# Fetching the basis matrices of a graph network base by base, in whole blocks, instead of by strided transfers over all bases

## The chip, the cores and the metric

The kernel runs on one core of one Trainium2 chip. The metric is the device time of one execution in microseconds (us). The profiled execution has a span of its own, from the first to the last instruction, and a time of its own beside it.

## What is computed

The reference is four layers on 10000 nodes of width 512 with 5000 edges: a relational graph network of two layers, a mixture-of-experts feed-forward, a second graph network of four layers, and a quantized feed-forward. The change touches only what prepares the first of them. Its two relations use weights that are combined from 30 bases:

```
x = x + gnn(layernorm(x), edges, basis1, att1, ..., basis2, att2, ...)
def rgcn_gate_layer(x, row, col, edge_type, basis, att, gate_w, root, bias):
    w = jnp.einsum('rb,bio->rio', att, basis)      # att 2x30, basis 30x512x512, w 2x512x512
```

There are two such tensors of bases (one for each layer), each 30 x 512 x 512 floats, 31.5 MB; together 62.9 MB that have to come from DRAM once.

## The kernel before

The kernel is a chain of phases with a barrier of all engines between them. The change is in the first large one, `front_phase` (line 230), which does three things side by side:

- It normalizes the rows of the input: `load(g)` (line 355) fetches 256 rows (512 KB) into one of four buffers, VectorE takes their statistics (`stats`, line 474, through `row_stats`, line 149), GpSimd makes the factors (`rstd`, line 317), ScalarE applies them and stores 512 KB to `normed` (`norm`, line 384). There are 40 such groups, the last of 16 rows.
- It sorts the edges by node, in 40 turns on TensorE, VectorE and GpSimd (`counts`, `turn_hot` and `look` from line 577, `advance` and `ranks` on VectorE, `scatter` on GpSimd).
- It combines the bases: for each of the two layers the 512 rows are cut into 8 blocks of 64 rows (`SIDE`, `BLOCKS`), 16 blocks in all. A block of all 30 bases lies in the on-chip memory with 120 partitions: base b has the partitions 4b to 4b+3, and partition 4b+q holds the rows q, q+4, q+8, ... of the block. Sixteen matrix products (`term`, line 548, one for each of the 16 rows of a partition) add up into one bank (`cb_ps`), the stationary operand (`spread`) putting row 4k+q of both relations in its place. ScalarE and VectorE split the result into a high and a low part (`block_high`, `block_low`), and ScalarE's queue stores both, 256 KB each.

SyncE issues all loads in an order written out by hand (lines 332 to 365). A block of bases comes as two halves, a half as four transfers, one for each quarter q: each reads, of all 30 bases, 8 rows that stand four rows apart, and writes 30 partitions that stand four apart, 480 KB in pieces of 2 KB. There are 32 halves in four buffers, so 128 transfers. A half waits (line 350) until the block that used its buffer is done. After the first four halves, each turn of the loop issues the load of one group of input rows, which waits for the `norm` of the group three before (line 357), and then on average 0.7 halves:

```
    src_ = networks[n][0].rearrange("b (j k q) o -> j b q k o", j=BLOCKS, q=4)[b]
    for quarter in range(4):
        eng.dma_start(ba_t[i % W][quarter:BASIS_ROWS:4, :, :], src_[:, quarter, half * HALF:(half + 1) * HALF, :]).then_inc(ba[i % W], 16)
```

TensorE's order is written by hand too: the 16 terms of block 0, the histogram of the edges, the terms of block 1, and then in every turn of the sort some 5.6 terms (lines 563 to 603). It waits for the bases at the first term of each half (line 550). ScalarE's queue has the stores of `normed` and of the combined weights (lines 392 and 404). After the sort SyncE reads back the sorted table (line 370), and the phase ends some 10 us later; the next phase, `relation_phase`, starts with its own loads (line 735 on).

Other transfers that the text behind this section speaks of: the loads of the edge lists on 125 partitions (line 336), the store of the gate's probabilities from 16 partitions (line 1119), the load of the edge terms on 5 partitions (line 1711), and the loads of the combined weights (line 743).

Of the kernel before, what the change touches and what calls it, by code (L numbers as in the profile page):

```python
# [10 lines left out]
P = 128  # L11
N, D, E = 10000, 512, 5000
KC = D // P
RELATIONS, BASES = 2, 30
# [7 lines left out]
ET = -(-E // P)  # L22
# [6 lines left out]
def wait(eng, sem, value):  # L29

    if not isinstance(value, int) or value > 0:
        eng.wait_ge(sem, value)  # L32
# [191 lines left out]
SIDE = 64  # L224
SHARE = SIDE // 4
BASIS_ROWS = 4 * BASES
BLOCKS = D // SIDE

def front_phase(core, ed, cst, src, dst, kind, weight, rows_in, normed, networks, combined):  # L230
# [6 lines left out]
    W = 4  # L237
# [2 lines left out]
    names = ("ld0 ld1 ld2 ld3 st0 st1 stats aggr var rstd nb norm "  # L240
             "ints rows hilo hot hist histc scan off base put "
             "count turned ohT look val rank made zdone tab fin1 wide place heads lasts merged "
             "att0 att1 ba0 ba1 ba2 ba3 cb chi clo cs0 cs1 sw0 sw1")
    with core.phase("order", names) as (s, sbuf, psum):
        load_i = sbuf("load_i", [P, 5, ET], I32)
        col = sbuf("col", [P, 5, ET])
# [29 lines left out]
        mv = [sbuf(f"mv{q}", [P, TILES, 2]) for q in range(W)]  # L276
        rs, ng, nb = ([sbuf(f"{n}{q}", [P, TILES]) for q in range(W)] for n in ("rs", "ng", "nb"))
        ld, st = [s[f"ld{q}"] for q in range(W)], [s[f"st{q}"] for q in range(2)]
        HALF = SHARE // 2
        ba_t = [sbuf(f"basis{q}", [BASIS_ROWS, HALF, D]) for q in range(W)]  # L280
        spread = [sbuf(f"spread{n}", [BASIS_ROWS, P + SIDE - 4]) for n in range(2)]
        c_hi, c_lo = [sbuf(f"c_hi{q}", [P, D], F32R) for q in range(2)], [sbuf(f"c_lo{q}", [P, D], F32R) for q in range(2)]
        ba, cs = [s[f"ba{q}"] for q in range(W)], [s["cs0"], s["cs1"]]
        ct_ps = [psum(f"ct_ps{q}", [HI, D]) for q in range(2)]
        c_ps = [a[:, 0:KEYS * P].rearrange("a (k p) -> a k p", k=KEYS) for a in ct_ps]
        turn_ps = [a[:, KEYS * P:KEYS * P * 3 // 2].bitcast(BF16).rearrange("a (k p) -> a k p", k=KEYS) for a in ct_ps]
# [8 lines left out]
        cb_ps = [psum(f"cb_ps{q}", [P, D]) for q in range(2)]  # L295
# [7 lines left out]
        with nc.Block() as block:  # L303
            @block.gpsimd
            def _(eng):
                eng.memset(load_i[:, 0:2, :], PAD_NODE)
                eng.memset(load_i[:, 2, :], RELATIONS)
                eng.memset(load_i[:, 3:5, :], 0)
                eng.memset(wt[:, :], 0.0)
                for n in range(2):  # L310
                    eng.memset(spread[n][:, :], 0.0)
                for k in range(KEYS):
                    eng.memset(row_i[k][:, E:EP], PAD_NODE)
                eng.memset(ones[:, :], 1.0)
                eng.memset(zeros[:, :], 0.0).then_inc(s["made"], 1)

                def rstd(g):
                    q = g % W
                    n, k = (REST, 1) if last(g) else (P, TILES)
                    wait(eng, s["norm"], g - W + 1)  # L320
                    row_rstd(eng, s, g, mv[q], cst.half, rs[q], last(g))
                    eng.wait_ge(s["rstd"], g + 1)
                    eng.tensor_tensor(nb[q][0:n, 0:k], ng[q][0:n, 0:k], rs[q][0:n, 0:k], ALU.mult).then_inc(s["nb"], 1)

                def scatter(t):
                    eng.wait_ge(s["rank"], t + 1)
                    for k in range(KEYS):
                        eng.indirect_dma_start(ed.table[k], bass.IndirectOffsetOnAxis(ap=ix[:, k, t:t + 1], axis=0),
                                               packed[:, k, t, :], None).then_inc(s[f"sw{k}"], 16)
                static_pipeline([(0, rstd), (2, scatter)], ET)  # L330

            @block.sync
            def _(eng):
                eng.wait_ge(s["made"], 1)
                for j, a in enumerate((src, dst, kind, src, dst)):
                    eng.dma_start(load_i[0:USED, j, :], a.rearrange("(p t) -> p t", t=ET)).then_inc(s["ints"], 16)
                eng.dma_start(wt[0:USED, :], weight.rearrange("(p t) one -> p (t one)", t=ET)).then_inc(s["ints"], 16)
                for n, (_, att) in enumerate(networks):
                    for r in range(RELATIONS):
                        for quarter in range(4):  # L340
                            at = SIDE - 4 + r * SIDE + quarter
                            eng.dma_start(spread[n][quarter:BASIS_ROWS:4, at:at + 1], att[r].rearrange("(b one) -> b one", one=1),
                                          allow_slow_non_contiguous=True).then_inc(s[f"att{n}"], 16)
                for k in range(KEYS):
                    eng.dma_start(row_i[k][:, 0:E], key_in[k].partition_broadcast(P)).then_inc(s["rows"], 16)
                eng.dma_start(ed.sums[1][ZERO_ROW:SUM_ROWS, :], zeros[:, :]).then_inc(s["zdone"], 16)

                def basis(i):
                    n, b, half = i // (2 * BLOCKS), i // 2 % BLOCKS, i % 2
                    wait(eng, s["cb"], (i - W) // 2 + 1 if i >= W else 0)  # L350
                    src_ = networks[n][0].rearrange("b (j k q) o -> j b q k o", j=BLOCKS, q=4)[b]
                    for quarter in range(4):
                        eng.dma_start(ba_t[i % W][quarter:BASIS_ROWS:4, :, :], src_[:, quarter, half * HALF:(half + 1) * HALF, :]).then_inc(ba[i % W], 16)

                def load(g):
                    q = g % W
                    wait(eng, s["norm"], g - W + 1)
                    eng.dma_start(part(x[q], last(g)), rows(rows_in, g, last(g))).then_inc(ld[q], 16)
                halves = 2 * 2 * BLOCKS
                for i in range(W):  # L360
                    basis(i)
                for t in range(ET):
                    load(t)
                    for i in range(min(halves, W + halves * t // ET), min(halves, W + halves * (t + 1) // ET)):
                        basis(i)

                for k in range(KEYS):
                    eng.wait_ge(s[f"sw{k}"], 16 * ET)
                for k in range(KEYS):
                    eng.dma_start(tabT[:, k, :, :], ed.table[k].rearrange("(t p) c -> t p c", p=P)).then_inc(s["tab"], 16)  # L370
                eng.wait_ge(s["tab"], 16 * KEYS)
                eng.wait_ge(s["wide"], KEYS)
                for k in range(KEYS):
                    eng.dma_start(ed.key_row[k].rearrange("(t p) -> t p", p=P), lineT[:, k, :]).then_inc(s["fin1"], 16)
                eng.wait_ge(s["wide"], KEYS + 2)
                for j, row in enumerate((weight_hi.ap().bitcast(F32), weight_lo.ap().bitcast(F32), weight_hi.ap().bitcast(F32),
                                         ones.ap(), ones.ap())):
                    eng.dma_start(ed.weight_rows[j].rearrange("(t p) -> t p", p=P), row).then_inc(s["zdone"], 16)
                eng.wait_ge(s["zdone"], 16 * (1 + TERMS))
                eng.wait_ge(s["fin1"], 16 * KEYS)  # L380
# [165 lines left out]
            @block.tensor  # L546
            def _(eng):
                def term(n, b, k):
                    j, half = n * BLOCKS + b, k // HALF
                    if k % HALF == 0:  # L550
                        i = 2 * j + half
                        eng.wait_ge(ba[i % W], (i // W + 1) * 64)
                    if k == 0:
                        if b == 0:
                            eng.wait_ge(s[f"att{n}"], 16 * RELATIONS * 4)
                        wait(eng, s["clo"], j - 1)
                    at = SIDE - 4 - 4 * k
                    m = eng.matmul(cb_ps[j % 2][:, :], spread[n][:, at:at + P], ba_t[(2 * j + half) % W][:, k % HALF, :],  # L558
                                   start=k == 0, stop=k == SHARE - 1)
                    if k == SHARE - 1:  # L560
                        m.then_inc(s["cb"], 1)
# [4 lines left out]
                for k in range(KEYS):  # L566
                    for t in range(ET):
                        m = eng.matmul(h_ps[:, k, :], hot_hi[k][:, t, :], hot_lo[k][:, t, :], start=t == 0, stop=t == ET - 1)
# [4 lines left out]
                for k in range(KEYS):  # L573
                    m = eng.matmul(o_ps[:, k:k + 1], cst.after[0:HI, 0:HI], incl[:, k, P - 1:P], start=True, stop=True)
# [30 lines left out]
                for k in range(KEYS):  # L605
                    m = eng.transpose(w_ps[:, k, :], apart[:, k, :], cst.ident[0:HI, 0:HI])
# [4 lines left out]
                for k in range(KEYS):  # L611
                    m = eng.matmul(m_ps[:, k, ET:ET + 1], shift[:, :], lineT[:, k, P - 1:P], start=True, stop=True)
                m.then_inc(s["lasts"], 1)
                for k in range(KEYS):
                    for c in range(3):
                        m = eng.transpose(t_ps[:, k, c, :], tabT[:, k, :, c], cst.ident[0:ET, 0:ET])
# [844 lines left out]
def routed_phase(core, cst, rows_in, w1, b1, w2, b2, token, score, routed):  # L1461
# [4 lines left out]
    K = HID + 1  # L1466
    HALF = SL * TPE // 2 + 2 - SL * TPE // 2 % 2
    names = ("w whi wlo ix T hi lo hm act gh gl one O ev "
# [934 lines left out]
```

## Time and profile before

| | |
|---|---|
| median of 3 runs | 5509.27 us (5506.63 to 5516.06) |
| profiled execution: time | 5506.21 us |
| profiled execution: span | 5504.4 us |
| mean granted TensorE clock | 0.827 |
| TensorE (matmul) busy | 4216.8 us, 77% of the span |
| VectorE, ScalarE, GpSimd busy | 2992.2, 2139.4, 1455.9 us |
| bytes moved by DMA | 924.32 MB, mean 168 GB/s |
| the phase of the change | from the start to about 463 us |

The profile's page cuts the span into 40 slices of 137.6 us; the phase of the change fills the first three and a third. A busy digit is in tenths. The DMA share is that of the core's 16 DMA engines, each packet counted for the time from its start to its end. In a row of a timeline the first number is the start, the second the duration. KB are of 1024 bytes, MB and GB of powers of ten.

### The profile page before, as it was taken

How to read it: one execution, taken by the hardware profiler on the slowest of the kernel's cores; microseconds unless marked ns; L12 is line 12 of the kernel's file. 1: busy time of each engine (PE TensorE's matmuls, PEld its weight loads, DVE VectorE, ACT ScalarE, POOL GpSimd, SP SyncE). 2: the span in 40 equal slices, each digit the busy share in tenths (PEclk: the TensorE clock that was granted, in tenths of full speed). 3: DMA queues.
4: the chain of work that ended last, by engine and by line, in shares of the span. 5: the costliest groups of instructions: out<-in, count | busy, mean ns of one | idle time of the engine just before them, and what ended most of it. 6: DMA issues, size and time to landing. Idle time of an engine off the chain costs nothing. (4 is left out here: it accounts for less than half of the span.)

```text
span 5504.4 us, 70253 instructions
## 1 busy us (share of the span) xinstructions
PE 4216.8 (77%) x22571; PEld 3378.6 (61%) x22571; DVE 2992.2 (54%) x6700; ACT 2139.4 (39%) x3450; POOL 1455.9 (26%) x1380
## 2 busy tenths in 40 slices
PE   5766989799897710663389897989889897989533
PEld 2334868688786610542179773988579774988311
DVE  3435754377685564434755445554455435554588
ACT  0111213222337800220133564347533664347566
POOL 1322112211340007774433004310233004310243
PEclk9887999899998855665589995999789995999755
DMA  8994237722896603666955226532555127532354
GB/s 235 295 273 152 77 114 250 238 72 71 330 401 244 235 20 90 121 127 157 330 177 162 76 94 231 162 112 91 194 171 162 72 96 234 162 106 92 136 195 161
DMA packets 493679, 924.32 MB, mean 168 GB/s; under 512 B 107759, under 2 KB 108039, under 8 KB 492632
## 3 DMA queue, kind: packets, MB, share of 16 engines
q1 hardware_dynamic: 296076, 532.11, 29.2%
q0 software_dynamic: 118272, 237.34, 15.8%
q10 hardware_dynamic: 79088, 151.77, 7.6%
q8 instruction: 136, 2.23, 0.2%
q14 instruction: 107, 0.88, 0.0%
HBM read 597.24 MB, written 322.46 MB: 167 GB/s over the span
## 5 line engine op out<-in xcount | busy, mean ns | idle before, releaser
L684 PE MATMUL hidden_O<-hidden_xh,w_hi 128*128 128x256 f32 (+1 forms) x2560 | 728.8, 285 | 0.3 <-DVE hidden_xl L1057 0.2
L685 PE MATMUL hidden_O<-hidden_xh,w_lo 128*128 128x256 f32 (+1 forms) x2560 | 717.0, 280 | 0.0
L686 PE MATMUL hidden_O<-hidden_xl,w_hi 128*128 128x256 f32 (+1 forms) x2560 | 716.8, 280 | 0.0
L684 PE MATMUL output_O<-w_hi,output_hh 128*128 128x512 f32 (+1 forms) x1264 | 503.3, 398 | 56.5 <-DVE output_hl L1950 56.5
L1829 POOL DMA_INDIRECT hidden_agg<-edge_sums,edge_where x316 | 339.6, 1075 | 756.8 <-DVE hidden_xin L1876 605.6
L1860 ACT ACTIVATE hT<-hidden_O,hidden_b 128x256 f32<-128x256 f32 (+1 forms) x640 | 247.6, 469 | 659.1 <-PE hidden_O L686 659.1
L685 PE MATMUL output_O<-w_hi,output_hl 128*128 128x512 f32 (+1 forms) x1264 | 502.4, 397 | 0.0
L686 PE MATMUL output_O<-w_lo,output_hh 128*128 128x512 f32 (+1 forms) x1264 | 502.1, 397 | 0.0
L684 PEld LDWEIGHTS hidden_O<-hidden_xh,w_hi 128*128 128x128 f32 x2560 | 484.4, 189 | 1.5 <-DVE hidden_xl L1057 1.4
L685 PEld LDWEIGHTS hidden_O<-hidden_xh,w_lo 128*128 128x128 f32 x2560 | 485.2, 190 | 0.0
L686 PEld LDWEIGHTS hidden_O<-hidden_xl,w_hi 128*128 128x128 f32 x2560 | 483.3, 189 | 0.0
L1956 DVE TENSOR_TENSOR output_y<-output_O,output_b2t 128x1024 f32<-128x1024 f32 (+1 forms) x160 | 193.7, 1211 | 510.9 <-PE output_O L686 510.9
L1882 DVE BATCH_NORM_STATS2 h_stats<-hT 128x6 f32<-128x256 f32 (+1 forms) x640 | 221.1, 408 | 447.0 <-ACT hT L1860 447.0
L1732 POOL DMA_INDIRECT message_x<-g,edge_partner x160 | 174.5, 1091 | 821.8 <-issue 722.0
L558 PE MATMUL order_cb_ps<-order_basis,order_spread 120*128 120x512 f32 x512 | 269.2, 680 | 79.1 <-DMA order_basis<-in_L_gnn_basis 79.1
L1966 ACT ACTIVATE hT<-hT,output_shf,output_scl (+2 forms) x640 | 326.7, 581 | 0.0
L684 PEld LDWEIGHTS output_O<-w_hi,output_hh 128*128 128x128 f32 (+1 forms) x1264 | 237.6, 188 | 116.1 <-issue 56.7
L686 PEld LDWEIGHTS output_O<-w_lo,output_hh 128*128 128x128 f32 (+1 forms) x1264 | 237.4, 188 | 60.3
L685 PEld LDWEIGHTS output_O<-w_hi,output_hl 128*128 128x128 f32 (+1 forms) x1264 | 237.7, 188 | 59.8
L1774 PE MATMUL message_X<-message_attr_terms,message_edge_terms 5*128 5x512 f32 x160 | 125.1, 787 | 186.8 <-DMA message_attr_terms<-edge_attr_rows 183.2
L684 PE MATMUL root_O<-root_hi,root_xh 128*128 128x512 f32 (+1 forms) x632 | 254.1, 402 | 0.0
L684 PE MATMUL relation_B<-w_hi,relation_pth 128*128 128x512 f32 x640 | 253.6, 396 | 0.0
(376 smaller groups left out, 10014.4 us busy)
## 6 DMA issues: line engine op xcount, KB each, us to landing
hidden_xin<-g SPq DMA_DIRECT2D x156, 512.0 KB, 4.0
g<-output_y SPq DMA_DIRECT2D x156, 512.0 KB, 2.7
order_basis<-in_L_gnn_basis SPq DMA_DIRECT2D x128, 480.0 KB, 16.5
edge_sums<-message_res SPq DMA_DIRECT2D x160, 256.0 KB
edge_sums<-relation_res SPq DMA_DIRECT2D x80, 256.0 KB, 2.0
order_x<-in_x SPq DMA_DIRECT2D x39, 512.0 KB, 17.9
normed<-order_y ACTq DMA_DIRECT2D x39, 512.0 KB, 9.2
root_xin<-normed SPq DMA_DIRECT2D x39, 512.0 KB, 3.7
```

What stands on the lines that cost most here:

```text
L558: m = eng.matmul(cb_ps[j % 2][:, :], spread[n][:, at:at + P], ba_t[(2 * j + half) % W][:, k % HALF, :], start=k == 0, stop=k == SHARE - 1)
L684: eng.matmul(out, a_hi, b_hi, start=start, stop=False)
L685: eng.matmul(out, a_lo, b_hi, start=False, stop=False)
L686: return eng.matmul(out, a_hi, b_lo, start=False, stop=stop)
L1732: eng.indirect_dma_start(x[t % R][:, :], None, table, bass.IndirectOffsetOnAxis(ap=ed.partner[1][:, t:t + 1], axis=0)).then_inc(ga[t % R], 16)
L1774: eng.matmul(X[t % 2][:, :], edge_terms[:, t * P:(t + 1) * P], attr_terms[:, :], start=True, stop=True).then_inc(s["E"], 1)
L1829: eng.indirect_dma_start(agg[j % R][0:n, :], None, ed.sums[1], bass.IndirectOffsetOnAxis(ap=ed.where[1][0:n, c:c + 1], axis=0)).then_inc(g ...
L1860: m = eng.activation(hT[:, o, at(g)], O[g % 2][:, o, 0:width_of(last(g))], ACT.Identity, bias=b1t[:, o:o + 1])
L1882: m = eng.bn_stats(stats[:, o, g, :], hT[:, o, at(g)])
L1956: eng.tensor_tensor(part(y[q], last), part(O[q], last), b2t[0:n, :].unsqueeze(1).to_broadcast([n, k, D]), ALU.add).then_inc(s["add"], 1)
L1966: m = eng.activation(hT[:, o, at(g, w_)], hT[:, o, at(g, w_)], ACT.Relu, bias=shf[:, o:o + 1], scale=scl[:, o:o + 1])
```

## The change

The buffers are two, each for a whole block, in place of four for half a block; their total size is the same. A block of bases is fetched by 30 transfers, one for each base, each of which reads 64 neighbouring rows of the base (128 KB in one piece of DRAM) and writes them to the four partitions of that base. There are 480 transfers in place of 128. A block waits once, at its first base, until the block before the last is done. The first two blocks are issued ahead of the first load of input rows; the other 14 are cut into 70 pieces of six transfers and spread evenly over the 40 turns. TensorE waits once per block, for all 30 transfers.

```diff
-        HALF = SHARE // 2
-        ba_t = [sbuf(f"basis{q}", [BASIS_ROWS, HALF, D]) for q in range(W)]
+        ba_t = [sbuf(f"basis{q}", [BASIS_ROWS, SHARE, D]) for q in range(2)]
...
-        ba, cs = [s[f"ba{q}"] for q in range(W)], [s["cs0"], s["cs1"]]
+        ba, cs = [s["ba0"], s["ba1"]], [s["cs0"], s["cs1"]]
...
-                def basis(i):
-                    n, b, half = i // (2 * BLOCKS), i // 2 % BLOCKS, i % 2
-                    wait(eng, s["cb"], (i - W) // 2 + 1 if i >= W else 0)
-                    src_ = networks[n][0].rearrange("b (j k q) o -> j b q k o", j=BLOCKS, q=4)[b]
-                    for quarter in range(4):
-                        eng.dma_start(ba_t[i % W][quarter:BASIS_ROWS:4, :, :], src_[:, quarter, half * HALF:(half + 1) * HALF, :]).then_inc(ba[i % W], 16)
+                def basis(j, b0, b1):
+                    n, i0 = j // BLOCKS, j % BLOCKS * SIDE
+                    if b0 == 0:
+                        wait(eng, s["cb"], j - 1)
+                    for b in range(b0, b1):
+                        eng.dma_start(ba_t[j % 2][4 * b:4 * b + 4, :, :],
+                                      networks[n][0][b, i0:i0 + SIDE, :].rearrange("(k q) o -> q k o", q=4)).then_inc(ba[j % 2], 16)
...
-                halves = 2 * 2 * BLOCKS
-                for i in range(W):
-                    basis(i)
+                pieces = [(j, b) for j in range(2, 2 * BLOCKS) for b in range(0, BASES, 6)]
+                for j in range(2):
+                    basis(j, 0, BASES)
                 for t in range(ET):
                     load(t)
-                    for i in range(min(halves, W + halves * t // ET), min(halves, W + halves * (t + 1) // ET)):
-                        basis(i)
+                    for j, b in pieces[len(pieces) * t // ET:len(pieces) * (t + 1) // ET]:
+                        basis(j, b, b + 6)
...
                 def term(n, b, k):
-                    j, half = n * BLOCKS + b, k // HALF
-                    if k % HALF == 0:
-                        i = 2 * j + half
-                        eng.wait_ge(ba[i % W], (i // W + 1) * 64)
+                    j = n * BLOCKS + b
                     if k == 0:
+                        eng.wait_ge(ba[j % 2], (j // 2 + 1) * 16 * BASES)
...
-                    m = eng.matmul(cb_ps[j % 2][:, :], spread[n][:, at:at + P], ba_t[(2 * j + half) % W][:, k % HALF, :],
+                    m = eng.matmul(cb_ps[j % 2][:, :], spread[n][:, at:at + P], ba_t[j % 2][:, k, :],
```

## Rows read from the trace of the kernel before

**Rows 1.** The page's slices: granted clock, DMA share and rate.
```profile
PEclk9887999899998855665589995999789995999755
DMA  8994237722896603666955226532555127532354
GB/s 235 295 273 152 77 114 250 238 72 71 330 401 244 235 20 90 121 127 157 330 177 162 76 94 231 162 112 91 194 171 162 72 96 234 162 106 92 136 195 161
```
**Rows 2.** Windows: length; PE, PEld, DVE, ACT, POOL busy; PE clock, DMA share, GB/s.
```profile
34.60:453.00 418.40, 305.03 (x918) 147.35 (x918) 165.26 (x710) 69.60 (x95) 117.58 (x160) 0.86 0.95 269
50.00:350.00 300.00, 233.91 (x719) 112.42 (x717) 116.78 (x494) 49.69 (x68) 81.17 (x112) 0.87 1.01 290
```
**Rows 3.** Waits of the engines in the window 34 to 453 us.
```profile
ACT order_y L389 <- DVE order_c_lo L481: 156.2, 13, 28.3
DVE order_bn L152 <- DMA order_x<-in_x: 124.5, 20, 15.9
PE order_cb_ps L558 <- DMA order_basis<-in_L_gnn_basis: 79.1, 13, 44.8
PE order_l_ps L593 <- DVE order_junk L461: 62.9, 15, 13.7
```
**Rows 4.** The page's DMA issues: queue, count, KB each, us to landing.
```profile
order_basis<-in_L_gnn_basis SPq DMA_DIRECT2D x128, 480.0 KB, 16.5
...
order_x<-in_x SPq DMA_DIRECT2D x39, 512.0 KB, 17.9
normed<-order_y ACTq DMA_DIRECT2D x39, 512.0 KB, 9.2
```
**Rows 5.** DMA issues of the whole trace: the first of four stores of combined weights.
```profile
combined1hi<-order_c_hi ACTq DMA_DIRECT2D x8, 256.0 KB, 7.9
```
**Rows 6.** DMA in 36 to 46 us, strided basis transfers alone.
```profile
DMA packets 1121, 2.15 MB, mean 215 GB/s; under 512 B 69, under 2 KB 69, under 8 KB 1121
...
q1 hardware_dynamic: 1121, 2.15, 98.2%
```
**Rows 7.** Window 1520 to 1570 us, 256-row transfers over 128 partitions; columns of Rows 2.
```profile
1520.00:1570.00 50.00, 50.00 (x255) 42.10 (x254) 42.06 (x73) 20.42 (x24) 22.45 (x32) 1.00 1.05 406
```
**Rows 8.** Timeline of SP's queue at 2693 us; DMA in 2694.7 to 2695.59 us.
```profile
2693.86 0.28 SPq L1711 DMA_DIRECT2D message_edge_terms<-edge_weight_rows  x1
...
DMA packets 5, 0.10 MB, mean 115 GB/s; under 512 B 0, under 2 KB 0, under 8 KB 0
...
q1 hardware_dynamic: 5, 0.10, 47.6%
```
**Rows 9.** Window 5.7 to 8 us, loads over 125 partitions landing; columns of Rows 2.
```profile
5.70:8.00 2.30, 0.00 (x0) 0.00 (x0) 0.00 (x0) 0.00 (x0) 0.00 (x0) 1.00 0.31 51
```
**Rows 10.** Store from 16 partitions: its issue; DMA in 1912.4 to 1919.9 us.
```profile
1912.05 0.33 SPq L1119 DMA_DIRECT2D probs<-tokens_pT  x1
...
DMA packets 41, 0.65 MB, mean 87 GB/s; under 512 B 23, under 2 KB 23, under 8 KB 24
...
q1 hardware_dynamic: 32, 0.64, 80.1%
```
**Rows 11.** Timeline: 16 issues of 128 KB each on SP's queue.
```profile
464.64 10.36 SPq L743 DMA_DIRECT2D w_hi<-combined1hi  x16
```
**Rows 12.** Timeline: one group's way from its statistics to its norm.
```profile
208.64 1.29 DVE L152 BATCH_NORM_STATS2 order_bn<-order_x 128x6 f32<-128x512 f32 x2 [8.02 <-DMA order_x<-in_x]
209.96 0.25 DVE L156 BATCH_NORM_AGGREGATE order_mv<-order_bn 128x2 f32<-128x6 f32 x2
...
210.63 0.72 POOL L171 TENSOR_TENSOR order_rs<-order_mv,cst_half 128x2 f32<-128x2 f32 x1 [8.12 <-DVE order_mv L163]
...
211.43 0.21 POOL L323 TENSOR_TENSOR order_nb<-order_ng,order_rs 128x2 f32<-128x2 f32 x1
...
223.50 1.52 ACT L389 ACTIVATE order_y<-order_x,order_nb,order_rs 128x512 f32<-128x512 f32 x2 [16.06 <-DVE order_c_lo L481]
```
**Rows 13.** Timeline: end of the sort and read-back of the table.
```profile
446.86 0.69 DVE L481 TENSOR_TENSOR order_c_lo<-order_cb_ps,order_c_hi 128x512 fp32r<-128x512 f32 x1 [1.74 <-ACT order_c_hi L398]
...
452.92 0.95 SPq L370 DMA_DIRECT2D order_tabT<-edge_table  x2
```

More of the change, by code:

```diff
@@ L242, in front_phase @@
              "count turned ohT look val rank made zdone tab fin1 wide place heads lasts merged "
-             "att0 att1 ba0 ba1 ba2 ba3 cb chi clo cs0 cs1 sw0 sw1")
+             "att0 att1 ba0 ba1 cb chi clo cs0 cs1 sw0 sw1")
     with core.phase("order", names) as (s, sbuf, psum):
```

## The prediction

> **What bounds the kernel now.** I read the page's slices first. In the first three the DMA engines are busy 8 to 9 tenths while the rate is only 235 to 295 GB/s [rows 1]. The windows of the phase say the same: from 34.6 us, when the first basis transfer runs, to 453 us the DMA share is 0.95 at 269 GB/s, and from 50 to 350 us it is 1.01 at 290 GB/s, while TensorE, the busiest compute engine, works 305 of 418 us [rows 2]. The waits agree: VectorE waits 124.5 us for input rows, TensorE 79.1 us for bases; ScalarE's 156.2 us behind VectorE's `c_lo` is the same delay handed on, since that follows the terms [rows 3]. So this phase is bound by transfers, and the phases are separated by barriers: what it gains or loses goes to the end one for one.
>
> The bytes can be counted. Bases: 128 x 480 KB = 62.9 MB. Input rows and `normed`: 39 x 512 KB and the short group, 20.5 MB each way [rows 4]. Combined weights: four tensors like the one shown, 32 x 256 KB = 8.4 MB [rows 5]. That is 112.3 MB, and 269 GB/s x 418.4 us is 112.5.
>
> Two rates are at work. When the strided basis transfers run alone, packets of 2 KB keep the engines 98.2% busy and yield 215 GB/s, 13.5 GB/s for each of 16 [rows 6]. Transfers of 2 KB pieces over all 128 partitions yield 406 GB/s at a full share, 25.4 GB/s for each [rows 7]. With these the phase adds up: 62.9 MB / 215 = 293 us, the other 49.4 MB / 406 = 122 us, together 415 us against 418.4 [rows 2]. I use this sum for the forecast, as it has just given the time before.
>
> **What the change does, part by part.**
>
> *How many engines serve a transfer.* This decides all. The trace shows engines going by the count of the outermost dimension, not by bytes. The edge terms, 100 KB on five partitions, go as exactly five packets, each on an engine of its own [rows 8]. The loads over 125 partitions fill 0.31 of 16 engines, which is five, the largest divisor of 125 up to 16 [rows 9]. A new basis transfer has four partitions outside on the one side and q = 4 on the other: I take four engines. If always the same four, they carry every base. The Trainium skill, "DMA: Bandwidth & Descriptors", section "Why a DMA increments its semaphore by 16 and not by 1", states both: the number is the largest up to 16 that divides the slowest dimension on both sides, and from SyncE it is the lowest-numbered ones. The five packets and the 0.31 agree; that it is the same four no row here shows.
>
> *The load on those four.* Each carries 62.9 / 4 = 15.73 MB of bases instead of about 4, beside its sixteenth of the rest, 49.4 / 16 = 3.09 MB, which at 25.4 GB/s takes 122 us as now [rows 7].
>
> *The rate of each.* Nothing before streams such transfers, so I bound it. Upper end: 25.4 GB/s [rows 7]. Lower end: the store from 16 neighbouring partitions, 640 KB by 16 packets that take 0.801 x 7.5 x 16 / 16 = 6.0 us each, 6.7 GB/s per engine [rows 10]. Between: the five packets, five neighbouring partitions, 0.476 x 0.89 us x 16 / 5 = 1.36 us for 20 KB, 15.1 GB/s [rows 8], and the strided stream with 13.5 [rows 6]. Few neighbouring partitions cost rate. I take 13.5: that row is nearest in size of piece, source and duration, and the five packets lie close to it. Then the bases take 15.73 MB / 13.5 GB/s = 1165 us instead of 293, +872 us. At 15.1 they take 1042 (+749), at 25.4 619 (+326), at 6.7 2348 (+2055).
>
> In the Trainium skill, "SBUF — State Buffer", section "Door 1: The DMA port swizzle", four neighbouring partitions share one port of about 27 GB/s, so that all four engines of a transfer meet there. By that alone a transfer moves 27 GB/s and the bases take some 2300 us; only engines that have drifted into different transfers get more. Rows 10 agree (four partitions to a port, 27 GB/s); rows 8 gave more than that in a short burst.
>
> *Issues.* SyncE issues 480 instead of 128. Sixteen issues of 128 KB took 10.36 us, 0.65 us each [rows 11], so 311 us. The transfers of at least 619 us cover that; if that cover were gone (all engines at work), 311 us plus the loads would be near the bound. Cost here: nothing.
>
> *Waits of TensorE: 16 instead of 32.* It can start a block only when all of it has landed, and its 305 us of work [rows 2] lie under transfers of over 1200. Now block 0 may start at the half. This costs nothing while the transfers are the bound, except at the end, where the terms of the last block follow the last landing; they do so now too. The `cb` wait of SyncE is the same in substance (a buffer is refilled when its block is done), and what stands behind it in SyncE's order, the loads of input rows, now waits in the same queue behind 30 transfers instead of 4.
>
> *The order.* The last basis piece of a block is issued two or three turns after the turn in which TensorE starts that block, and each turn's load waits for the `norm` three turns back. So where it is three (8 of the 14 blocks) TensorE must first reach the turn, VectorE, GpSimd and ScalarE must norm its group, before the last pieces go out. That chain is 1.3 + 0.3 + 0.7 + 0.2 + 1.5 = 4 us of work [rows 12], and with issue and the way there I take 8 us. In all but two of the blocks (counted from the two lists of turns) a piece of 0.8 MB is already queued beyond, which covers it. Two times 8 us: +16 us. Bounds: 0 and 14 x 8 = 112 us.
>
> *The tail.* Now SyncE's read-back of the table starts at 452.92, six us after the last block's `c_lo` [rows 13]. That stays behind the last block.
>
> **Sum.** 872 + 16 = +888 us on the profiled execution's 5506.2 us: 6394. Its time is 3 us under the median of the runs shown, which I leave out of account. About 0.2%, 11 us, is what a measurement here can tell from no change.
>
> **The rivals.**
>
> *The four engines run apart.* If the strided stream is slow for its strides in DRAM and not for where it writes, or if the four drift into different transfers, each gives 25.4 GB/s: +326 + 16, 5848 us. For it: the new reads are one piece of 128 KB. [...] Against: the five packets, whose source is dense, are slow too [rows 8].
>
> *They meet all the time.* 6.7 GB/s each: +2055 + 16, 7577 us. For it: the order is the same on all four, and each drained queue lines them up again. Against: 15.1 in rows 8. A mixture, lined up at each block and apart after, lies between 6394 and this.
>
> *The transfers spread over all engines.* This ends faster. The place is how the 64 rows are dealt out; it decides from the point where the bases move at over 215 GB/s, which at 25.4 each needs nine engines. Then bases take 62.9 / 406 = 155 us, the rest 122, in all 277, and the next bound is SyncE's issues, 311 us and 40 loads of 0.4 us (of the size of those in rows 8 and 10): 327 instead of 415, 5418 us. For it: the bytes of a transfer are one piece in DRAM and could be cut anywhere. Against: rows 8 and 9.
>
> *The change does nothing to the time*: the engines number about nine, or the transfers are hidden; against it speaks a DMA share of 0.95 [rows 2]. 5506 us.
>
> **How the numbers follow.** Four engines at 13.5 to 15: 0.45. Apart: 0.25. Always meeting, or nearly: 0.17. Spread: 0.10. Nothing: 0.03. The forecast is the likeliest, 6394 us. The range begins just under the second case, 5830, and ends at 7300, inside the mixtures towards the third; outside stay the spread, the unchanged and the worst meeting, about 0.2. Faster 0.10, same 0.03, slower 0.87.
>
> **What would show it.** Right: the phase ends near 1340 us; in its slices the DMA share falls from 0.95 to some 0.3 while its rate falls to some 90 GB/s; TensorE's wait for `order_basis` grows from 79 to many hundred us; SyncE's basis issues stretch over the whole phase, x480 of 128 KB; the phases behind keep their length. A window with only bases shows a share near 0.25: that is the four engines; its GB/s over four is their rate, 13.5 by the forecast, 25.4 or 6.7 by the rivals. Wrong at the first step would be a share near 1 there.

## The result and the profile after

The changed kernel takes 6083.17 us (median of 4 runs, 6071.82 to 6090.84) against 5512.67 us of the kernel before in the same series: a ratio of 1.103, 95% interval 1.100 to 1.105, or 570 us slower. The forecast was 6394 us, range 5830 to 7300, with 0.87 on slower. The profiled execution took 6071.82 us; its span is 6070.0.

The page's slices of the changed kernel, 151.8 us each, to be read beside [rows 1]. In the first six and a half the DMA share is 3 to 4 tenths where it was 8 to 9, and the rate 106 to 137 GB/s:

```profile
DMA  3433334227722987225769542554255424552354
GB/s 106 136 110 116 123 114 137 73 83 247 237 73 87 392 323 271 81 71 118 128 161 321 161 135 85 186 167 134 88 177 173 143 85 166 181 149 80 121 185 166
```

Windows of the changed kernel: the phase up to the last bases, a stretch near its start with bases alone, one a little later, and a stretch of the next phase (columns of [rows 2]):

```profile
34.60:1012.00 977.40, 295.72 (x910) 143.44 (x911) 159.49 (x688) 68.29 (x93) 112.42 (x155) 0.67 0.36 114
...
36.00:46.00 10.00, 0.00 (x0) 0.00 (x0) 0.00 (x0) 0.00 (x0) 0.00 (x0) 1.00 0.26 30
60.00:100.00 40.00, 9.20 (x16) 4.05 (x17) 0.00 (x0) 0.00 (x0) 0.00 (x0) 1.00 0.26 97
...
1060.00:1160.00 100.00, 98.16 (x495) 83.44 (x496) 73.83 (x212) 25.58 (x43) 17.05 (x14) 0.96 0.24 78
```

The same bytes as before, 114 GB/s x 977 us = 111 MB, take 977 us instead of 418. With bases alone the share is 0.26 of 16 engines: four engines. The trace's semaphore events say the same: the 240 transfers into one buffer raise its semaphore 1200 times, five each: once at the issue and then once for each of four engines. That share of 0.26 holds through 60 transfers issued one behind the other. Had different transfers gone to different fours, more would have been busy at a time, so it is always the same four; that is inferred, as no packet names its engine. The phase behind runs as it did (78 GB/s; 79 in the same stretch before). The read-back of the sorted table, at 452.92 us before [rows 13], is at 1020.01: 567 us later, which is all of the difference.

The longest waits of the phase, to be read beside [rows 3]. TensorE now waits 716.3 us for bases instead of 79.1, and VectorE and GpSimd, whose share of each turn stands behind TensorE's, wait with it:

```profile
POOL order_rs L171 <- DVE order_mv L163: 858.9, 39, 146.9
PEld order_cb_ps L556 <- DMA order_basis<-in_L_gnn_basis: 725.4, 16, 90.8
PE order_cb_ps L556 <- DMA order_basis<-in_L_gnn_basis: 716.3, 16, 90.8
DVE order_ohT L470 <- PE order_ct_ps L583: 699.7, 39, 60.3
ACT order_y L389 <- DVE order_c_lo L481: 435.2, 13, 65.1
```

What the forecast did not have is in the DMA view of 36 to 76 us, one figure for each microsecond. The share doesn't move, but the rate begins at 27 GB/s, stays near 30 for 12 us and then climbs to 98:

```profile
DMA  2232222222222222222222222222222222222222
GB/s 27 25 31 39 29 27 25 41 31 25 29 47 39 37 53 78 78 76 86 76 90 74 92 78 96 78 94 92 92 98 96 92 98 94 90 96 86 98 88 94
```

So the four engines deliver anything from 7 to 25 GB/s each on the same kind of transfer. The semaphore events of the slow part show them in step: the four completions of a transfer land together, at 40.18 to 40.24 us and again at 44.30 to 44.64; from 47 us on they no longer come in fours. The slow part comes back after most pauses of the queue. This is such a pause, from the timeline of the changed kernel (start and duration in us):

```profile
415.40 3.70 SPq L352 DMA_DIRECT2D order_basis<-in_L_gnn_basis  x3
421.09 5.49 PE L556 MATMUL order_cb_ps<-order_basis,order_spread 120*128 120x512 f32 x6 [45.89 <-DMA order_basis<-in_L_gnn_basis]
...
430.83 0.68 DVE L481 TENSOR_TENSOR order_c_lo<-order_cb_ps,order_c_hi 128x512 fp32r<-128x512 f32 x1
...
432.47 1.52 ACT L389 ACTIVATE order_y<-order_x,order_nb,order_rs 128x512 f32<-128x512 f32 x2 [56.64 <-DVE order_c_lo L481]
...
434.02 0.39 SPq L358 DMA_DIRECT2D order_x<-in_x  x1
```

SyncE has issued all that it may at 419.10. The block that TensorE waits for is in at 421.09. Only then can the sort's turn go on, VectorE write `c_lo` of the block before, ScalarE, which stands behind it, norm a group at 432.47, and SyncE go on at 434.02. Fifteen us without a new transfer; by the packets of SyncE's queue, all four engines have nothing left from 428.4 to 435.0. This happens nine times in the phase, for 4.5 to 11.1 us and 63 us in all (three times and 18 us in the kernel before). The rate from 434 to 474 us, with the input rows' 244 to 410 GB/s at first, is then 43 to 91 for 14 us before it climbs (the 154 to 242 are input rows again):

```profile
GB/s 12 66 244 406 410 345 78 27 248 251 68 53 58 91 70 60 70 57 43 66 84 76 74 86 78 154 242 170 70 82 92 86 88 94 90 96 98 100 129 268
```

SyncE's waits for `norm` over the phase (46.7 us in the kernel before):

```profile
SPq L358 <- ACT order_y L389: 144.3, 11, 19.4
```

### The profile page after: what moved, and what is told of

Read it like the earlier page. It is cut to its first block and busy times, and to the rows that moved or that the text cites. A ratio compares the mean times of both kernels' runs of the same rounds, so it can differ in the third digit from the quotient of the medians.

```text
span 6070.0 us, 70605 instructions
## 1 busy us (share of the span) xinstructions
PE 4192.8 (69%) x22571; PEld 3360.7 (55%) x22571; DVE 2993.9 (49%) x6700; ACT 2142.7 (35%) x3450; POOL 1457.5 (24%) x1380
## 5 line engine op out<-in xcount | busy, mean ns | idle before, releaser
L556 PE MATMUL order_cb_ps<-order_basis,order_spread 120*128 120x512 f32 x512 | 266.9, 674 | 716.3 <-DMA order_basis<-in_L_gnn_basis 716.3
L556 PEld LDWEIGHTS order_cb_ps<-order_basis,order_spread 120*128 120x128 f32 x512 | 106.8, 218 | 843.1 <-DMA order_basis<-in_L_gnn_basis 725.4
L470 DVE CAST order_ohT<-order_ct_ps 80x256 f32<-80x256 bf16 x40 | 16.8, 420 | 699.7 <-PE order_ct_ps L583 699.7
L389 ACT ACTIVATE order_y<-order_x,order_nb,order_rs 128x512 f32<-128x512 f32 (+1 forms) x79 | 60.1, 808 | 761.9 <-DVE order_c_lo L481 435.2
```

## The experiments

My theory (A) after reading this: the loss has three parts. Four engines instead of sixteen; their meeting at the four neighbouring partitions that they all write, which begins anew after every pause and ends as they drift into different transfers; and the pauses. The rival (B): the slow stretches belong to the source in DRAM or to starting up. The next two experiments change one of these each.

### Pieces three turns earlier

```diff
-                    for j, b in pieces[len(pieces) * t // ET:len(pieces) * (t + 1) // ET]:
+                    for j, b in pieces[len(pieces) * (t + 3) // ET if t else 0:min(len(pieces), len(pieces) * (t + 4) // ET)]:
```

> The changed kernel with every piece of the bases issued three turns earlier in SyncE's order (a block still waits until the block before the last is done). Theory A, the four engines meet on one place in the on-chip memory after each pause and drift apart while their queues stay full: the pauses before the starts of blocks go, so there is only the slow stretch at the very beginning. Of the 977 us that the bases took, 741 are the four engines at 25.4 GB/s, 236 are pauses and slow stretches; some 200 of them go: about 5880 us, and the DMA share no longer falls to 0 between blocks. Rival B, the slow stretches belong to the transfers or to the source in DRAM and not to the pauses: only the pauses go, at least 6000 us.

Measured: 5901.61 us, ratio 1.071 (1.069 to 1.072); 182 us less than the changed kernel. The first stretch is nearly as slow as before, since nothing there has changed; its DMA rate in 36 to 46 us is 40 GB/s. After it SyncE hardly waits for `norm` any more (10.0 us; 144.3 in the changed kernel), its queue never runs dry, and the slow restarts are gone. The row from the waits of its queue:

```profile
SPq L358 <- ACT order_y L389: 10.0, 7, 2.6
```

The slow stretches follow the pauses, so they don't belong to the transfers. As A had it; the time is 22 us over its figure.

### The four partitions of a base four apart

Base b has the partitions 16 (b / 4) + b mod 4 + 4q in place of 4b + q. Eight partitions among the 128 then hold zeros, which VectorE writes once, and the factors of `spread` come in more and smaller loads, on ScalarE's queue.

```diff
-        ba_t = [sbuf(f"basis{q}", [BASIS_ROWS, SHARE, D]) for q in range(2)]
+        ba_t = [sbuf(f"basis{q}", [P, SHARE, D]) for q in range(2)]
...
-                        eng.dma_start(ba_t[j % 2][4 * b:4 * b + 4, :, :],
+                        p0 = b // 4 * 16 + b % 4
+                        eng.dma_start(ba_t[j % 2][p0:p0 + 13:4, :, :],
```

> The changed kernel, same transfers and same order, but the four partitions of a base stand four apart (16 partitions for four bases) instead of next to each other. Theory A, the four engines of a transfer meet because they write four neighbouring partitions: now they don't, so 36 to 46 us shows about 100 GB/s at a share of 0.25 instead of 30 GB/s, and each restart too; the pauses stay. Some 150 us less: about 5930 us. Rival B, the slow starts come from the DRAM side or from starting up: 36 to 46 us stays at about 30 GB/s and the time at about 6080 us.

Measured: 5946.55 us, ratio 1.078 (1.076 to 1.080), 137 us less than the changed kernel. The DMA view of the same 36 to 76 us, the same reads by the same four engines:

```profile
DMA  2222222222222222222222222222222222222222
GB/s 98 98 100 98 98 100 98 102 98 98 98 98 98 98 100 102 98 100 98 98 98 98 100 100 100 102 102 98 102 102 98 102 102 98 100 100 102 98 102 100
```

98 GB/s all along. This is not the stream's beginning, though: with the factors' loads gone from SyncE's queue, its bases start at about 23 us, 11 us earlier than in the changed kernel. They rise to 98 GB/s in 6 us, where the changed kernel takes some 30. The restarts decide it. This is 262 to 302 us, after 11 us without anything in the queue; the queue fills again at 264.8, and past the burst of input rows the rate is near 100 and never under 76:

```profile
GB/s 262 264 14 98 307 410 406 360 102 209 388 101 104 100 88 99 101 102 162 268 209 76 100 100 102 98 100 102 100 98 102 102 98 98 102 102 164 309 148 84
```

The reads are the same and the queue still runs dry nine times, 63 us in all, so rival B is out, and what slows the four engines is shown: that they write four neighbouring partitions at one time. Of the 137 us some 11 are the earlier start. By the Trainium skill, "SBUF — State Buffer", section "Door 1: The DMA port swizzle", four neighbouring partitions share one port of about 27 GB/s, and the first figures here are 27 and 25.

### Both together

> The changed kernel with both edits, pieces three turns earlier and the four partitions of a base four apart. Theory A, pauses and meetings are all that lies between the 741 us of four engines at 25.4 GB/s and what was measured: 741 us instead of the 415 of the kernel before, and a little at both ends, 5840 to 5880 us. Rival B, a third loss remains (the queue of SyncE, the order of the loads): no better than the earlier pieces alone, 5895 us or more.

Measured: 5873.21 us, ratio 1.066 (1.064 to 1.067). The phase from the first bases to the end of the last (columns of [rows 2]):

```profile
34.60:812.00 777.40, 328.30 (x916) 158.09 (x916) 168.07 (x701) 70.06 (x95) 113.84 (x157) 0.71 0.41 143
```

777 us against 741 (619 for the bases and 122 for the rest) of four engines that never meet nor pause. So no third loss of size is left: the 570 us are about 360 for having four engines (some 370, as this kernel too starts its bases 11 us earlier), and 200 to 210 for pauses and meetings. The two don't add up. Taking the meetings away is worth 137 us while there are pauses (6083 to 5947) but 28 without (5902 to 5873), the 11 us of the earlier start in both. The pauses are worth 182 us while the engines meet but 73 when they don't. The 73 us are close to the 63 for which the queue is dry. Some 110 us are the meetings that a pause sets off.

### Two bases per transfer

The transfer has 8 partitions on one side and 2 bases on the other. To keep it to three dimensions a partition now holds neighbouring rows (16q + k in place of 4k + q, in the stationary operand too).

```diff
-                    for b in range(b0, b1):
-                        eng.dma_start(ba_t[j % 2][4 * b:4 * b + 4, :, :],
-                                      networks[n][0][b, i0:i0 + SIDE, :].rearrange("(k q) o -> q k o", q=4)).then_inc(ba[j % 2], 16)
+                    for b in range(b0, b1, 2):
+                        eng.dma_start(ba_t[j % 2][4 * b:4 * b + 8, :, :],
+                                      networks[n][0][b:b + 2, i0:i0 + SIDE, :].rearrange("b (q k) o -> b q k o", q=4)).then_inc(ba[j % 2], 16)
```

> Two bases per transfer (256 KB in eight partitions, 240 transfers), each partition holding 16 neighbouring rows. If the engines go by the smaller outermost dimension (2 bases in DRAM, 8 partitions on chip): two engines, a share near 0.13 and at most 51 GB/s with bases alone; 31.5 MB per engine at 25.4 GB/s is 1239 us, so at least 6450 us. Rival, they go by the destination's 8 partitions: eight engines, a share near 0.5, and a time between 5500 and 5650 us.

Measured: 6453.77 us in one run. Bases alone (columns of [rows 2]):

```profile
36.00:46.00 10.00, 0.00 (x0) 0.00 (x0) 0.00 (x0) 0.00 (x0) 0.00 (x0) 1.00 0.12 52
```

Twice the bytes per transfer and twice the partitions, and half the engines: 0.12 of 16 is two. That is the count of bases; by the eight partitions it would have been eight. The semaphore events agree: three for each transfer, one at the issue and two engines'. The two write different groups of four partitions, and each gives its full 26 GB/s. By the rule in the Trainium skill, "DMA: Bandwidth & Descriptors", section "Why a DMA increments its semaphore by 16 and not by 1", the engines divide both dimensions, and 2 is what divides 8 and 2.

### Dense rows with four engines

The control for the kernel above: one base per transfer, 16 neighbouring rows (32 KB) per partition.

> The changed kernel with 16 neighbouring rows per partition: each of the four engines reads its own 32 KB piece in DRAM, where before their 2 KB rows alternated; destinations, engines and order are unchanged. Theory A, they meet at the destination: 36 to 46 us stays slow, under 50 GB/s, and the time within 60 us of the changed kernel's 6083. Rival B, they meet at the source, where four engines read alternate rows of one piece: near 100 GB/s at 36 to 46 us and a time near 5940 us.

Measured: 6040.59 us in one run, 43 us under the changed kernel, in a series whose kernel before was 14 us slower (5526.22); and 33 GB/s in 36 to 46 us:

```profile
36.00:46.00 10.00, 0.00 (x0) 0.00 (x0) 0.00 (x0) 0.00 (x0) 0.00 (x0) 1.00 0.21 33
```

The engines meet also when each reads a piece of its own. A second answer against the DRAM side, and within the 60 us that A allowed.

### One transfer per block, fifteen engines

Whole-block buffers and the earlier turns as in the first experiment, dense rows, and all 120 partitions at once.

```diff
-                    for b in range(b0, b1):
-                        eng.dma_start(ba_t[j % 2][4 * b:4 * b + 4, :, :],
-                                      networks[n][0][b, i0:i0 + SIDE, :].rearrange("(k q) o -> q k o", q=4)).then_inc(ba[j % 2], 16)
+                    if b1 == BASES:
+                        eng.dma_start(ba_t[j % 2][:, :, :],
+                                      networks[n][0][:, i0:i0 + SIDE, :].rearrange("b (q k) o -> b q k o", q=4)).then_inc(ba[j % 2], 16)
```

> The changed kernel's two whole-block buffers, the pieces' turns three earlier, but one transfer per block for all 120 partitions, each holding 16 neighbouring rows (32 KB in one piece). Outermost dimensions 120 and 30: 15 engines, a share of 0.94 or more with bases alone and over 200 GB/s there. The number of engines was then the whole loss: 5460 to 5530 us. Rival, waiting for whole blocks in two buffers costs of itself: 5560 us or more with the engines busy all the same.

Measured: 5563.97 us, ratio 1.009 (1.007 to 1.011): slower than before by some 50 us. The time is that of the rival (5560 us or more), not that of the number of engines alone. The share is near that of fifteen engines (0.94), the rate 199 GB/s:

```profile
36.00:46.00 10.00, 0.00 (x0) 0.00 (x0) 0.00 (x0) 0.00 (x0) 0.00 (x0) 1.00 0.95 199
```

So fifteen engines, with dense rows and one transfer per block, bring back 338 of the 388 us that the first experiment was slower than before. This run doesn't part the three; dense rows alone gave 43 us with four engines. The rest is not the whole-block wait alone: the kernel before with only that wait is the next experiment.

### The kernel before, waiting for whole blocks

```diff
-                    if k % HALF == 0:
-                        i = 2 * j + half
-                        eng.wait_ge(ba[i % W], (i // W + 1) * 64)
+                    if k == 0:
+                        for i in (2 * j, 2 * j + 1):
+                            eng.wait_ge(ba[i % W], (i // W + 1) * 64)
```

> The kernel before, but TensorE waits for both halves of a block at its first term. The prediction put this at nothing: within 10 us of the kernel before. Rival, TensorE then starts each block later and hands the delay on through the sort to the loads: 20 to 60 us slower.

Measured: 5518.59 us, ratio 1.0015 (1.0004 to 1.0026). It costs, but some 8 us only (interval 2 to 14), within the 10 that were expected. So the wait for whole blocks explains a small part of the 50 us of the one transfer.

### Is the kernel before held by meetings too?

This goes beyond the second experiment: no two of the fifteen write into the same four neighbouring partitions, and no run shows which engine would meet which. Four kernels ask what limits the stream. All have dense rows (the partition's rows are 16q + k) and half-block buffers, and fifteen engines but for the last:

- dense quarters: the transfers of the kernel before, 16 KB in one piece instead of eight rows of 2 KB;
- dense halves: one transfer for the four quarters, so that an engine stays 64 KB at the four partitions of a base;
- short stays: twice the transfers at half the size, 8 KB at a partition;
- ten apart: ten bases per transfer, partitions twelve apart, so ten engines. Here the factors' loads are on ScalarE's queue, and the first bases are issued at 8.4 us instead of 21.8.

```diff
-                    src_ = networks[n][0].rearrange("b (j k q) o -> j b q k o", j=BLOCKS, q=4)[b]
+                    src_ = networks[n][0].rearrange("b (j q k) o -> j b q k o", j=BLOCKS, q=4)[b]
...
-                    for quarter in range(4):
-                        eng.dma_start(ba_t[i % W][quarter:BASIS_ROWS:4, :, :], src_[:, quarter, half * HALF:(half + 1) * HALF, :]).then_inc(ba[i % W], 16)
+                    for k in range(0, HALF, 4):
+                        for quarter in range(4):
+                            eng.dma_start(ba_t[i % W][quarter:BASIS_ROWS:4, k:k + 4, :], src_[:, quarter, half * HALF + k:half * HALF + k + 4, :]).then_inc(ba[i % W], 16)
```

(The first two lines are the dense quarters, the rest the short stays.)

> The kernel before, with rows of a partition that are neighbours in DRAM: each transfer reads 16 KB in one piece from each of the 30 bases instead of eight rows 8 KB apart; partitions, engines and order unchanged. Theory A, the strided stream's 215 GB/s comes from engines that meet at their destinations: it stays near 215 GB/s in 36 to 46 us and the time within 15 us of the kernel before. Rival B, it comes from the stride of the rows in DRAM: up to 406 GB/s there, and a time of 5400 to 5440 us.

> The kernel before with dense rows, as in the dense quarters, and one transfer per half of a block instead of four (32 transfers of 1.9 MB). If number and size of the transfers don't matter beside the number of engines: as the dense quarters, 5460 to 5490 us. If the alternation of four small transfers helped the pairs of engines to drift apart: slower than that, 5490 to 5515 us.

> The dense quarters with twice as many transfers of half the size, so that an engine stays 8 KB instead of 16 KB at one group of four partitions before it goes to the next. If pairs of engines meet there and come apart sooner when the stays are short (16 KB stays: 5475 us; 64 KB stays: 5556 us): at or under 5475 us, 5440 to 5475. Rival, more and smaller transfers cost SyncE and the engines more than that: 5480 us or more.

> The kernel before with dense rows and ten bases per transfer, twelve partitions apart: ten engines, which by the rule of the partitions drawn from the second experiment never meet. Theory A: bases alone show a share of 0.63 and 254 GB/s from the first one on, above the 215 of fifteen engines in pairs; other transfers keep sixteen engines, so each of the ten carries 6.3 MB of bases and 3.1 MB of the rest, 370 us instead of 415: 5460 to 5490 us. Rival, the pairs were not what held the fifteen: ten give two thirds of 215, about 145 GB/s, and the time is 5600 us or more.

| | median, us | ratio to before (95%) | 36 to 46 us, nearly all bases | 50 to 350 us |
|---|---|---|---|---|
| before | 5512.88, 5509.57, 5526.22 in the three series | | 215 GB/s | 290 GB/s |
| dense halves, 64 KB stays (second series) | 5556.20 | 1.008 (1.007 to 1.010) | 205 | 266 |
| dense quarters, 16 KB (first) | 5474.59 | 0.993 (0.992 to 0.995) | 229 | 321 |
| short stays, 8 KB (third) | 5470.75 | 0.990 (0.989 to 0.992) | 269 | 323 |
| ten apart (third) | 5534.19 | 1.002 (1.000 to 1.003) | 262 | 278 |

The windows of 50 to 350 us, of the dense halves, the dense quarters and the short stays:

```profile
50.00:350.00 300.00, 225.15 (x680) 108.67 (x678) 110.79 (x468) 46.04 (x63) 75.59 (x105) 0.87 0.98 266
```
```profile
50.00:350.00 300.00, 241.96 (x784) 118.86 (x783) 132.39 (x563) 57.78 (x79) 92.92 (x128) 0.90 0.98 321
```
```profile
50.00:350.00 300.00, 244.18 (x785) 120.26 (x784) 135.66 (x578) 58.35 (x80) 93.92 (x131) 0.90 0.97 323
```

From 36 to 46 us, the dense quarters and the short stays:

```profile
36.00:46.00 10.00, 1.41 (x2) 0.83 (x3) 0.00 (x0) 0.00 (x0) 0.00 (x0) 1.00 0.98 229
```
```profile
36.00:46.00 10.00, 3.21 (x4) 1.51 (x5) 0.00 (x0) 0.00 (x0) 0.00 (x0) 1.00 0.96 269
```

And ten engines that by theory A never meet, with bases alone but for some tiny loads of factors:

```profile
36.00:46.00 10.00, 10.00 (x25) 4.40 (x24) 0.00 (x0) 1.28 (x1) 0.00 (x0) 1.00 0.64 262
```

Ten engines deliver more than fifteen: 26 GB/s each at a share of 0.64, in all 262 against 229 with the same dense pieces of 16 KB. So fifteen get in each other's way and ten, twelve partitions apart, don't. That they do so where they write is what the second experiment suggests; with fifteen instead of ten, though, there are also more reads at once, and no run here tells the two apart. What it is worth in time is not as A had it. The ten-apart kernel was to take 5460 to 5490 us and took 5534, which misses the rival's 5600 too. Its share of 0.79 from 50 to 350 us is not short of work: by my estimate ten full engines, and six that carry only their sixteenths of the 49.4 MB, a third of the time, make 0.75. Only behind that does the share fall, to 0.65 from 400 to 430 us. Why stays open; SyncE's 384 issues at 0.75 us are 288 us, and it waits 37 us for `norm` and 76 us for blocks to be done.

The dense quarters hit neither expectation: 229 GB/s at the start, near A's 215, but 38 us gained where A had less than 15 and B at least 70. Dense rows and meetings may both have a part in it, and these runs don't separate them. The dense halves hit neither of theirs: 5556 us, where the slower of the two ended at 5515. The short stays came in at 5471, inside 5440 to 5475. Shorter stays give the higher rates at the start, as A has it (205, 229, 269 GB/s), but from 16 to 8 KB the time hardly changes.

One thing grows against it, ScalarE's wait for its own store of a group, here for the short stays (8 KB pieces), the dense quarters (16 KB), the dense halves (16 KB) and the one transfer (32 KB), after the kernel before (2 KB):

```profile
ACT order_y L389 <- DMA normed<-order_y: 60.2, 9, 8.2
```
```profile
ACT order_y L390 <- DMA normed<-order_y: 80.2, 13, 12.1
```
```profile
ACT order_y L389 <- DMA normed<-order_y: 135.1, 23, 13.0
```
```profile
ACT order_y L388 <- DMA normed<-order_y: 212.4, 28, 18.2
```
```profile
ACT order_y L389 <- DMA normed<-order_y: 270.9, 25, 22.5
```

The ten-apart kernel, with 16 KB pieces too, has 99.6 us, so the size of the pieces is not all of it. I take this wait for what made the one transfer and the dense halves slower than before, beside the long stays: the norms come later, and SyncE's loads wait for them, 201 and 248 us in these two against 46.7 in the kernel before. But the dense quarters wait 121 us and are faster than before. No run changed the size of the pieces alone, so this is argued from the waits and not shown.

The short stays and the dense quarters are the fastest kernels of this study, 0.990 and 0.993 of the kernel before. Their intervals overlap.

## Why the prediction was right, and where it was off

- **What bounds the phase.** Right. The phase is bound by transfers and its loss goes to the end one for one: 567 us at the read-back, 570 in the time. The phase ended at some 1020 us and not near the 1340 of the forecast.
- **How many engines.** Right: four, and the same four. The share of 0.26, the two engines with two bases, the fifteen of the one transfer all go by the same rule.
- **The rate of each.** This is the term that was mis-sized. I took 13.5 GB/s from the strided stream and so 1165 us for the bases (that stream has fifteen engines and not sixteen, so even there it was 14.3). Over the phase the kernel took 977 us for bases and all else, where the sum had 1287. Less 122 us for the rest and 63 us with a dry queue that leaves about 790 for the bases, 20 GB/s each on average. The rate is no constant: it is 7 GB/s when the four are lined up on one transfer, 25 when they have come apart, and it was near 25 for the larger part of the time. I had written that only engines that drifted into different transfers get more; I gave the case in which they do 0.25 and should have asked how fast they get there, which is 15 to 25 us. The kernel before misled: its fifteen engines stayed at 215 GB/s in the whole stretch that I read [rows 6], and I took that for what engines do that meet.
- **The pauses.** I had put two of 8 us, 16 in all, with bounds of 0 to 112. Without meetings they cost 73 us, within the bounds; with them 182. Three steps were off. The first is their number: I had all but two covered by a piece already queued, and the queue ran dry nine times. The second is the way from a landed block to the next issue: it takes 13 us (421.09 to 434.02), not 8. I had left out the six terms that stand before the turn; they take 5.49 us, as TensorE, idle for 45.89 us before, runs at a granted clock of 0.57 from 421 to 428 us, near the lower of its two levels (1.2 of 2.4 GHz), while the ten terms behind the turn take 4.46. And ScalarE's norm stands behind the stores of the block before, whose `c_lo` comes first in its order. The third is the price: a pause costs more than its length, since it lines the engines up again; the prediction names that only under the rival of constant meeting.
- **Issues and TensorE's waits.** Nothing for both. That is right for the issues: the first 60 took 98 us, 1.6 each where I had 0.65, because the queue took them no faster than the engines carried them, and later SyncE stood waiting for `norm`. For the waits it was 8 us, measured in the kernel before.
- **The rivals.** The result, 6083, lies between the case apart (5848) and the forecast. With both losses taken away the kernel reached 5873, 25 us over that case's figure. That the forecast came within 311 us is in part luck: the 13.5 GB/s are the rate of no stretch of this kernel, they only happen to lie between its 7 and 25, and the pauses, put too low, took back some 50 of the 370 us by which the bases were put too high. Spreading over all engines did not happen; when it was made to happen, the time came to within 50 us of before, not to the 5418 that I had given it.

## What to carry to other kernels

In all these runs a transfer was carried by as many engines as divide the outermost dimensions of both its sides (4 and 4: four; 8 and 2: two; 120 and 30: fifteen), and a small one there, like four partitions or two bases, caps the whole stream however many transfers are queued; the DMA share in a stretch with nothing else shows the number, if roughly. Contiguous reads didn't make up for that. Then look at where the engines write at one time: four engines on neighbouring partitions ran at 27 GB/s where 98 were possible, keeping the queue full let them come apart, and most drained queues brought the loss back, so a short pause in front of such a stream is dearer than it looks.

## What was not expected of the hardware

- Four engines on the same queue with equal shares drift apart by themselves: 27 GB/s at 36 us, 78 at 51 us, 96 at 60 us, 101 near 100 us. The fifteen of the kernel before gain nothing in that way: 205 to 238 GB/s from 36 to 70 us.
- Four partitions that stand four apart take 98 GB/s within 6 us of the stream's start and at once after a pause, four neighbouring ones 27 at first, with the same source and the same number of engines.
- Ten engines with partitions twelve apart (262 GB/s) beat fifteen (229 GB/s with the same pieces, 215 with strided rows).
- With pieces of 8, 16 and 32 KB in one queue the total wait for the 2 KB pieces of another was 80, 100 to 212, and 271 us, against 60 with 2 KB pieces. No run changed the size alone.
